# Squared attention scores: value product in fp32 instead of three fp16 products, the square formed from the score bank

## The reference, cut to what matters

```
queries, keys, values = l2norm(queries), l2norm(keys), l2norm(values)
sim  = einsum('bhid,bhjd->bhij', queries, keys)
attn = square(relu(sim))
aggr = einsum('bhij,bhjd->bhid', attn, values)
out  = tanh_norm(aggr) * tanh(silu(gates))
return out @ Wout
```

## Time and profile before

| | |
|---|---|
| median of 3 runs | 3120.21 us (3118.69 to 3121.61) |
| profiled execution | span 3118.2 us; its own time about 2 us more, as the runs' median is 2.0 above the span |
| TensorE matmul busy | 2774.7 us, 15168 records |
| VectorE busy | 2549.5 us, 5207 instructions |
| ScalarE busy | 2288.4 us, 4138 instructions |
| GpSimd busy | 888.1 us, 683 instructions |
| granted clock of TensorE, mean | 0.976 |

### The profile page before, as it was taken

How to read it: one execution, slowest core, us unless ns; L and a number is a source line. 1 busy time by engine, 2 the same in 40 slices (tenths; PEclk the granted TensorE clock), 3 DMA queues, 4 the chain that set the end, 5 groups by cost and what they waited for, 6 DMA issues and landing times.

```text
span 3118.2 us, 54633 instructions
## 1 busy us (share of the span) xinstructions
PE 2774.7 (89%) x15168; PEld 1174.7 (38%) x15168; DVE 2549.5 (82%) x5207; ACT 2288.4 (73%) x4138; POOL 888.1 (28%) x683
## 2 busy tenths in 40 slices
PE   2898998989989899998989989899898998989999
PEld 1343343333433344333433334333343333434433
DVE  8987879778687887878878788786987879888796
ACT  3787767778677786877868678686776867778686
POOL 0314123141332413224132231412314123141332
PEclk8999999999999999999999999999999999999999
DMA  3000000000000000000000000000000000000000
GB/s 154 7 1 21 1 22 1 1 22 1 22 1 1 22 1 22 1 1 22 1 22 1 1 22 1 22 1 22 1 1 22 1 22 1 1 22 1 14 1 8
DMA packets 19501, 40.23 MB, mean 13 GB/s; under 512 B 1584, under 2 KB 9904, under 8 KB 18128
## 3 DMA queue, kind: packets, MB, share of 16 engines
q1 hardware_dynamic: 19152, 36.11, 3.4%
HBM read 27.72 MB, written 8.39 MB: 12 GB/s over the span
## 4 chain that ended last, share of the span: by engine, by line
PE 40%; DVE 35%; issue 14%; ACT 7%; DVEq 2%; POOL 1%; ACTq 0%; DMA 0%; SPq 0%; POOLq 0%
PE wk L1104 18%; DVE pl L589 10%; PE acc L1104 10%; DVE ph L585 7%; PE av L1177 5%; DVE wide L505 2%; PE sim L1163 2%; ACT ring L899 2%; PE wk L1186 2%; DVE hf L609 2%; DVE vn_t L418 1%; ACT ring L903 1%; ACT sg L909 1%; PE wk L1228 1%; DVE vn_y L420 1%
## 5 line engine op out<-in xcount | busy, mean ns | idle before, releaser
L1056 POOL TENSOR_TENSOR hl<-hf,hh 128x512 f16<-128x512 f32 x288 | 369.5, 1283 | 1645.8 <-ACT hh L915 1482.0
L589 DVE TENSOR_TENSOR pl<-ring,ph 128x512 f16<-128x512 f32 x1024 | 759.9, 782 | 0.0
L899 ACT ACTIVATE ring<-sim 128x512 f32<-128x512 f32 x1024 | 567.5, 603 | 250.3 <-PE sim L1163 176.6
L903 ACT ACTIVATE ring<-ring 128x512 f32<-128x512 f32 x1024 | 593.6, 640 | 0.0
L585 DVE CAST ph<-ring 128x512 f16<-128x512 f32 x1024 | 472.0, 497 | 83.0 <-ACT ring L903 54.3
L1177 PE MATMUL av<-ph,vh 128*64 128x512 f16 x1024 | 211.7, 410 | 42.5 <-DVE pl L589 42.4
L609 DVE SCALAR_TENSOR_TENSOR hf<-wk,up_routed,sg 128x512 f32<-128x512 f32 x256 | 191.6, 749 | 66.9 <-PE wk L1104 16.3
L909 ACT ACTIVATE sg<-wk,inv_m 128x512 f32<-128x512 f32 x288 | 199.6, 693 | 46.6 <-PE wk L1104 46.4
L1077 POOL TENSOR_TENSOR pl<-wide,ph 128x512 f16<-128x512 f32 x128 | 169.6, 1329 | 211.4 <-ACT ph L947 211.4
L641 DVE TENSOR_TENSOR gate_sb<-gate_sb,wk 128x512 f32<-128x512 f32 x128 | 87.8, 686 | 162.9 <-PE wk L1228 162.7
L1104 PE MATMUL acc<-hh,down_h 128*128 128x512 f16 x576 | 220.2, 382 | 0.0
(11 more groups left out here) (192 smaller groups left out, 5386.4 us busy)
## 6 DMA issues: line engine op xcount, KB each, us to landing
x_sb<-x SPq DMA_DIRECT2D x16, 512.0 KB, 4.9
y_sb<-x_t SPq DMA_DIRECT2D x16, 512.0 KB, 4.3
out_t<-y_sb SPq DMA_DIRECT2D x16, 512.0 KB, 3.2
raw_wa<-wa SPq DMA_DIRECT2D x1, 2560.0 KB, 9.1
raw_gate<-w_gate SPq DMA_DIRECT2D x1, 2304.0 KB, 14.2
raw_up<-w_up SPq DMA_DIRECT2D x1, 2304.0 KB, 19.3
raw_down<-w_down SPq DMA_DIRECT2D x1, 2304.0 KB, 24.3
raw_wo<-w_out SPq DMA_DIRECT2D x1, 1024.0 KB, 26.1
```

The source lines that it names most:

```text
L589: v.tensor_tensor(pl[:, n % NH_, :], ring[:, n % NR_, :], ph[:, n % NH_, :], ALU.subtract).then_inc(pl_done, 1)
L899: a(ring[:, n % NR_, :], sim[n % 2][:, :], ACT.Relu, scale=S_SCALE).then_inc(relu_done, 1)
L903: a(ring[:, n % NR_, :], ring[:, n % NR_, :], ACT.Square).then_inc(square_done, 1)
L1056: tt(hl[:, n % 2, :], hf[:, n % 2, :], hh[:, n % 2, :], ALU.subtract).then_inc(h_lo, 1)
```

## The change

The square is formed on VectorE in one instruction: the score, read from its PSUM bank, times the rectified score from `ring`, to fp32 in a new tensor `pf`. ScalarE's square and VectorE's cast and subtraction go. The values stay in fp32 (`vf`), without cast and subtraction, and the value product is one fp32 matmul a head. The scale of the square changes from 2^14 to 2^21, since only one of its factors has been scaled by the rectifier. The score bank is held until the multiplication: `scores` now waits for `pf_done` where it waited for `relu_done`. The raw values no longer share their place with the heads' results, so their two waits for the previous batch's output moved to `take_heads`.

```diff
@@ VectorE
             def probs(b, n):
-                dve.wait_ge(square_done, upto(b, 2 * STEPS, n + 1))
+                dve.wait_ge(relu_done, upto(b, 2 * STEPS, n + 1))
                 dve.wait_ge(av_step, upto(b, STEPS, n // 2 - LAG))
-                if n < 4:
+                if n < 2:
                     dve.wait_ge(out_mm, upto(b, NP_, 0))
-                v.tensor_copy(ph[:, n % NH_, :], ring[:, n % NR_, :]).then_inc(ph_done, 1)
-
-            def probs_lo(b, n):
-                dve.wait_ge(ph_done, upto(b, 2 * STEPS, n + 1))
-                v.tensor_tensor(pl[:, n % NH_, :], ring[:, n % NR_, :], ph[:, n % NH_, :],
-                                ALU.subtract).then_inc(pl_done, 1)
+                v.tensor_tensor(pf[:, n % NH_, :], sim[n % 2][:, :], ring[:, n % NR_, :],
+                                ALU.mult).then_inc(pf_done, 1)
@@ ScalarE
-            def split_hi_v(b, n):
-                k, half = n // 2, n % 2
-                act.wait_ge(vn_done, upto(b, 2 * NB, n + 1))
-                act.wait_ge(av_step, upto(b, STEPS, 0))
-                a(vh[:, k, half * T:half * T + T], v_raw[:, k, half * T:half * T + T], ACT.Copy).then_inc(v_hi, 1)
...
-            def square(b, n):
-                act.wait_ge(relu_done, upto(b, 2 * STEPS, n + 1))
-                a(ring[:, n % NR_, :], ring[:, n % NR_, :], ACT.Square).then_inc(square_done, 1)
@@ GpSimd
-            def split_lo_v(b, n):
...
-                tt(vl[:, k, sl], v_raw[:, k, sl], vh[:, k, sl], ALU.subtract).then_inc(v_lo, 1)
@@ TensorE, scores
-                    pe.wait_ge(relu_done, upto(b, 2 * STEPS, n - 1))
+                    pe.wait_ge(pf_done, upto(b, 2 * STEPS, n - 1))
@@ TensorE, values
-                pe.wait_ge(pl_done, upto(b, 2 * STEPS, 2 * s + 2))
+                pe.wait_ge(pf_done, upto(b, 2 * STEPS, 2 * s + 2))
                 if pair == 0:
-                    pe.wait_ge(v_lo, upto(b, 2 * NB, 2 * (j + 1)))
+                    pe.wait_ge(vn_done, upto(b, 2 * NB, 2 * (j + 1)))
...
-                for i, (vv, pp) in enumerate(((vh, ph), (vl, ph), (vh, pl))):
-                    for half in range(2):
-                        h = 2 * pair + half
-                        ins = mm(av[64 * half:64 * half + 64, :], vv[:, j, h * DV:(h + 1) * DV],
-                                 pp[:, (2 * s + half) % NH_, :], start=(j == 0 and i == 0),
-                                 stop=(j == NB - 1 and i == 2))
+                for half in range(2):
+                    h = 2 * pair + half
+                    ins = mm(av[64 * half:64 * half + 64, :], vf[:, j, h * DV:(h + 1) * DV],
+                             pf[:, (2 * s + half) % NH_, :], start=(j == 0), stop=(j == NB - 1))
```

More of the change, by code:

```diff
@@ L38 @@
 S_SCALE = 2.0 ** -7
-P_SCALE = 2.0 ** 14
+P_SCALE = 2.0 ** 21
 V_SCALE = 2.0 ** 8
@@ L239, in build_layer @@
         y_sb = sb("y_sb", [P, KD, T])
-        ph, pl = sb("ph", [P, NH_, T], F16), sb("pl", [P, NH_, T], F16)
+        pf = sb("pf", [P, NH_, T])
+        ah, al = (pf[:, c, :].bitcast(F16).rearrange("p (n t) -> p n t", n=2) for c in range(2))
         wide = sb("wide", [P, NP_, T])
-        v_raw = wide[:, :, :].rearrange("p (k a) t -> p k (a t)", k=NB)
         agg = wide
@@ L245, in build_layer @@
         qt, kt = sb("qt", [P, NP_, T], F16), sb("kt", [P, NP_, T], F16)
-        vh, vl = sb("vh", [P, NB, H * DV], F16), sb("vl", [P, NB, H * DV], F16)
+        vf = sb("vf", [P, NB, H * DV])
         sg = sb("sg", [P, 2, T])
@@ L269, in build_layer @@
         work_full = sem("work_full")
-        sim_full, relu_done, square_done = sem("sim_full"), sem("relu_done"), sem("square_done")
-        ph_done, pl_done, av_step = sem("ph_done"), sem("pl_done"), sem("av_step")
+        sim_full, relu_done = sem("sim_full"), sem("relu_done")
+        pf_done, av_step = sem("pf_done"), sem("av_step")
         agg_done, agg_sq_done = sem("agg_done"), sem("agg_sq_done")
@@ L503, in unit_v @@
                 dve.wait_ge(raw_done, upto(b, 3 * NB, NB + n + 1))
-                blk = v_raw[:, k, half * T:half * T + T].rearrange("p (h d) -> p h d", d=DV)
+                blk = vf[:, k, half * T:half * T + T].rearrange("p (h d) -> p h d", d=DV)
                 v.scalar_tensor_tensor(out=blk, in0=blk, scalar=V_SCALE,
@@ L779, in body @@
                         expert_item(b, kind, e)
-                    for n in (2 * s, 2 * s + 1):
-                        probs_lo(b, n)
                     if not last:
@@ L838, in raw @@
                 if n < NB:
-                    act.wait_ge(pl_done, upto(b, 2 * STEPS, 0))
+                    act.wait_ge(pf_done, upto(b, 2 * STEPS, 0))
                     dst = qk_raw[:, n, :]
@@ L842, in raw @@
                     k, half = (n - NB) // 2, (n - NB) % 2
-                    act.wait_ge(a_hi, upto(b - 1, NP_, n - NB + 1))
-                    act.wait_ge(a_lo, upto(b - 1, NP_, n - NB + 1))
-                    dst = v_raw[:, k, half * T:half * T + T]
+                    act.wait_ge(av_step, upto(b, STEPS, 0))
+                    dst = vf[:, k, half * T:half * T + T]
                 a(dst, bank(b, key)[:, :], ACT.Copy).then_inc(raw_done, 1)
@@ L886, in turned_k @@
                   ACT.Copy).then_inc(k_turned, 1)
[L888 to L892 removed]
             def relu(b, n):
                 act.wait_ge(sim_full, upto(b, 2 * STEPS, n + 1))
[L896 removed]
+                act.wait_ge(pf_done, upto(b, 2 * STEPS, n - NR_ + 1))
                 if n < NR_:
@@ L931, in take_heads @@
                 act.wait_ge(av_step, upto(b, STEPS, NB * (t + 1)))
-                act.wait_ge(v_lo, upto(b, 2 * NB, 2 * NB))
-                act.wait_ge(v_hi, upto(b, 2 * NB, 2 * NB))
+                act.wait_ge(a_hi, upto(b - 1, NP_, t + 1))
+                act.wait_ge(a_lo, upto(b - 1, NP_, t + 1))
                 a(agg[:, t, :], av[:, :], ACT.Copy).then_inc(agg_done, 1)
@@ L985, in whole @@
                         relu(b, n)
-                    for n in (2 * s, 2 * s + 1):
-                        square(b, n)
                     for kind, e in PLAN[s]:
@@ L1043, in split_lo_qk @@
                     tt(lo, src, hi, ALU.subtract).then_inc(qk_lo, 1)
-            def split_lo_v(b, n):
-                k, half = n // 2, n % 2
-                pool.wait_ge(v_hi, upto(b, 2 * NB, n + 1))
-                pool.wait_ge(av_step, upto(b, STEPS, 0))
-                sl = slice(half * T, half * T + T)
-                tt(vl[:, k, sl], v_raw[:, k, sl], vh[:, k, sl], ALU.subtract).then_inc(v_lo, 1)
             def body(b, last):
@@ L1060, in body @@
                 hidden_lo(0)
-                for n in range(2):
-                    split_lo_v(b, n)
                 for s in range(STEPS):
@@ L1066, in body @@
                             hidden_lo(ORDER.index(e) - 1)
-                    if s in (1, 2, 3):
-                        split_lo_v(b, 2 * s)
-                        split_lo_v(b, 1 + 2 * s)
                 for kind, e in TAIL:
```

7 lines of the change are left out of this document (removed).

## The result

The changed kernel takes 3168.82 us (median of 4 runs, 3161.93 to 3171.51) against 3119.66 us before (now 4 runs): ratio 1.0154, 95% interval 1.0139 to 1.0168. It is 49 us slower.

What follows compares the result with a forecast made beforehand. TensorE's work was taken as 108.7 of a batch's 123.5 us of steps, the rest waits, mostly VectorE's. Longer value products (+19.8), waits and half clock gave 138.5, less 0.4: +14.6 a batch, +234 over sixteen, 3355 us; range 3170 to 3545.

Steps and rivals of the forecast that it cites:

- how the two heads overlap: Value product on TensorE: second head's records start behind the first's, group 1.39 us instead of 0.77, +19.8 us a batch.
- The price of a record: Value product: each fp32 record of 512 columns holds its columns for 0.43 us, twice the fp16 time.
- the count of 2048 records: Sign to look for: the value product's records in the profile number 2048 in fp32.
- the forecast's 138.5: The 32 score steps of one batch: 138.5 us with the change, against 123.5 before.
- The last batch: Counted as one of sixteen equal batches, each +14.6 us.
- the rest of the batch: Outside the steps: 0.4 us a batch earlier, without waits for the value halves on ScalarE; projections, tail and output unchanged.
- rival A: Value product: the two heads overlap fully, 0.96 us a group, 3150 us in all; chance 0.12.
- The argument against A: Value product: an fp32 product is two records, and matmuls start in program order, so heads cannot overlap fully.
- The relief: Less VectorE and ScalarE work in the steps: can give back at most 14.8 us of waits a batch, 237 in all.
- The held bank: Scores wait for the previous step's multiplication: 5.6 us a batch at the start, 1.4 in steps without enough cover.
- half clock: Steps of a batch: 1.0 us lost to TensorE running at half clock.
- The other engines: Busy time over the run: VectorE near 1900 us, ScalarE near 1600.

Runs made afterwards that it cites:

- e2_same_cols: Changed kernel with both heads of a step writing their value products to the same 64 columns: 3535.75 us, one run.
- e10: Changed kernel with the two heads' value products written on two source lines, same instructions otherwise: 3166.49 us, one run.
- e14: Changed kernel with the second head's fp32 value product replaced by one fp16 matmul into the same columns: 3125.52 us, one run.
- e6_ring_pad24: Changed kernel with the square formed from the ring alone, scores waiting for the rectifier only, and 24 small matmuls ahead of the first batch: 3026.74 us.
- e8: Kernel before, with VectorE forming the square from the ring straight to fp16 in one multiplication, low part left out: 2992.41 us.
- e4_pad24: Changed kernel with 24 small fp16 matmuls put once ahead of the first batch on TensorE: 3132.26 us.
- e7: As e6_ring_pad24, but ScalarE squares the rectified score into the fp32 tensor instead of VectorE: 3024.49 us.
- e12: As e4_pad24, but VectorE does the last six value norms two by two after the multiplications of steps 1, 2 and 3: 3109.98 us.

## Why the prediction was wrong

**The step that failed** is the one on how the two heads overlap: "B first is behind it in the queue and starts with it; B second starts at 0.86 and ends at 1.29". The price of a record was right (0.43 us by e2_same_cols), and so was the count of 2048 records. The order was not: the second head starts with the first (e10, e14), so the group takes 1.01 to 1.02 us, not 1.39. That is 0.37 x 512 = 189 us, and the forecast missed by 186. That the two agree so closely is chance. The steps came out 14.5 us a batch below the forecast's 138.5: 11.8 of that is the overlap, and 2.7 are waits that didn't come. The last batch came out better than forecast too (11 us slower, not 15), and the rest of the batch came out worse by 2.6 us (below). These nearly cancel.

The prediction had this case as its rival A, with 0.12, at 0.96 us a group. A's 3150 left out 0.06 us a group and the stall, which are 31 and 37 us, and had 11 us of waits a batch where 7.3 came (124.0 - 116.7). Without the stall the time would be 3132, well below the range that begins at 3170; that the measured time misses it by only 1 us is owed to the stall, and so to chance. The argument against A was in-order starts read off products with a single record each. The rows cited don't show the starts of the records within a product that has two.

By the Trainium skill, "TensorE: Matmul & The Clock Gate", section "Measured speedup vs the span model", packed tiles cost one duration; the starts 0.01 us apart in e10 agree with it for fp32. The same page's "What overlaps and what doesn't" has matmuls start and end in program order; e14 shows a product starting ahead of an earlier product's second record, so the order holds for the first records of products here, not for all records. By its row it also ends (1505.01 + 0.40) before that second record starts (1505.48), though ends are modelled in the profile. A semaphore on the product written last may then not cover the one before it; no run here tests that.

**The relief.** The prediction took TensorE's work without waits as 108.7 us a batch and all waits of the steps, 14.8, as open to be given back. With groups of 1.02 us the work is 108.7 + 8.0 = 116.7; e6_ring_pad24, without the held bank, takes 116.9. Of that, 0.7 are waits for the weighting (10.7 us in the run), so the work was counted right to about 0.5 us. But relief alone does not give back all the waits: e8, with the short groups, takes 114.2, so 9.5 of the 14.8 us came back (128 us over the run).

**The held bank.** Forecast 7.0 us a batch, 5.6 of them at the start and 1.4 in the up steps, and 1.0 of half clock. Measured: e4_pad24 has 6.2 us more a batch in its steps than e6_ring_pad24. The two differ in the bank and in what the multiplication reads (810 ns in the mean from the ring, 684 from the bank); e7, where VectorE doesn't multiply at all, has 116.6, so that hardly counts. The places were right, the sizes were not: in a batch at full clock 2.3 us at the start and 2.0 around steps 9, 20 and 29, and about 1.5 in the mean from batches that lost their clock at the start. The norms hold step 1's scores as forecast, for less time (3.69 us, not 4.80), but moving them gains nothing at full clock (e12).

**The rest of the batch** was forecast at -0.4 us and came out at +2.2: the stall after the jump, 37 us by e4. The sum had no term for it, and nothing in the profile before shows such a stall. Without it the change would have been slower by 0.4%.

**The last batch** was priced like all others. Its steps lost 11.3 us where a middle one's lost 0.3, since it had fewer waits to give back.

**The other engines** came out at 2014 and 1735 us busy, against about 1900 and 1600 forecast. Instructions that follow closely overlap in the rows (two multiplications of 0.68 us take 1.28), so a sum of durations is more than the busy time it removes. It had no effect on the time.

## What to carry to other kernels

Before pricing a wider product by the order of its passes, measure one group of it: here most of the miss was 0.37 us, repeated 512 times. Holding a PSUM bank for one more reader costs where the queue behind it is short, not where the engines are full: look for the shortest step, and free the bank by reading the copy that exists already. When instructions are added or removed ahead of a loop, compare the stretch after its jump back, and the instruction reads in part 3 of the page: a part of the code that nobody touched may move by a per cent, either way.

## What was not expected of the hardware

- Two fp32 products with 64 columns each run together as fp16 ones do: 1.01 us for both, 1.01 for one alone, 1.87 in the same columns.
- The stall after the loop's jump: none in the kernel before, 1.6 us at the twelfth matmul in the changed one, 3.4 us at the fifth with 8 matmuls more ahead of the loop, none with 24 or 64. The kernel's time went 3169, 3194, 3132, 3139 by that alone.
- A 16 KB read of instructions starts 1 to 3 us behind the jump, with the stall and without. Where TensorE stalls, it goes on 2.2 to 3.3 us after that read has started.
